# x1 transposed by VectorE in 32x32 blocks and sixteen SBUF transfers instead of by TensorE

## The reference

```python
x = L0_attn_x                                    # (16, 512, 256)
qkv = relu(x @ qkv_weight.T)                     # q, k, v: 32 heads of 8
vk = einsum('bnhe,bnhd->bhed', [v, 1], k)        # linear attention, per head
vk_q = einsum('bhed,bnhd->bnhe', vk, q)
att = vk_q[..., :8] / (vk_q[..., 8:] + 1e-15)
x1 = layernorm(x + att @ proj_weight.T + proj_bias)
h = silu(x1 @ (w_gate/127).T) * (x1 @ (w_up/127).T)      # hidden 768
out = layernorm(x1 + h @ (w_down/127).T)
```

## Time and profile before

| | |
|---|---|
| median of 3 runs | 555.05 us (554.89 to 556.29) |
| the profiled execution, its own time | 556.24 us |
| its span, first to last instruction | 554.4 us |
| mean granted TensorE clock | 0.995 |
| TensorE busy | 542.7 us (98%) |
| VectorE busy | 387.2 us (70%) |
| ACT busy | 221.3 us (40%) |
| GpSimd busy | 80.2 us (14%) |

### The profile page before, as it was taken

One profiled execution on the slowest core, in us unless ns is written; L12 is line 12 of the kernel. 1 busy time (PEld: TensorE's weight loads), 2 busy tenths in 40 slices (PEclk: granted clock), 3 DMA queues, 4 the chain that ended last, 5 costly groups with the idle time before them and its releaser, 6 DMA issues.

```text
span 554.4 us, 8767 instructions
## 1 busy us (share of the span) xinstructions
PE 542.7 (98%) x3275; PEld 480.0 (87%) x3275; DVE 387.2 (70%) x867; ACT 221.3 (40%) x376; POOL 80.2 (14%) x94
## 2 busy tenths in 40 slices
PE   8889999999999999999999999999999999999995
PEld 5778989898898988989898898988989898898975
DVE  5786758486684957758487684957858587684976
ACT  3356243543524445243542524445243442524431
POOL 1011110011110111110011110111110011100212
PEclk9999999999999999999999999999999999999999
DMA  8300121201111030121202112030121202102001
GB/s 302 154 0 2 39 77 40 76 0 76 38 38 76 0 113 0 38 76 38 76 0 76 38 38 76 0 113 1 38 76 38 76 0 76 38 0 77 2 39 38
DMA packets 8652, 29.02 MB, mean 52 GB/s; under 512 B 960, under 2 KB 1728, under 8 KB 8640
## 3 DMA queue, kind: packets, MB, share of 16 engines
q1 hardware_dynamic: 8640, 28.85, 14.4%
HBM read 20.46 MB, written 8.39 MB: 52 GB/s over the span
## 4 chain that ended last, share of the span: by engine, by line
PE 91%; DVE 4%; DMA 2%; ACT 1%; issue 1%; POOL 0%; SPq 0%; POOLq 0%
PE abcd_ps L580 48%; PE gate_ps L580 17%; PE up_ps L580 16%; PE abcd_ps L616 6%; PE abcd_ps L624 5%; DMA wg_raw<-w_gate 1%; DMA xT_raw<-x_chan 1%; DVE x1T_lo L336 0%; DVE h L343 0%; DVE xT_lo L336 0%; ACT silu L240 0%; DVE wg_lo L336 0%; DVE st L562 0%; DVE st L397 0%; DVE r L558 0%
## 5 line engine op out<-in xcount | busy, mean ns | idle before, releaser
L343 DVE SCALAR_TENSOR_TENSOR h<-up_ps,silu 128x512 f32<-128x512 f32 x96 | 66.0, 687 | 82.7 <-ACT silu L240 82.7
L240 ACT ACTIVATE silu<-gate_ps 128x512 f32<-128x512 f32 x96 | 57.4, 598 | 107.3 <-PE gate_ps L580 107.3
L580 PE MATMUL abcd_ps<-wd_hi,h_hi 128*128 128x256 f32 x384 | 93.1, 283 | 0.8 <-DVE h_lo L336 0.8
L580 PE MATMUL abcd_ps<-wd_hi,h_lo 128*128 128x256 f32 x384 | 92.9, 283 | 0.0
L580 PE MATMUL gate_ps<-x1T_hi,wg_hi 128*128 128x512 f32 x192 | 79.6, 415 | 2.0 <-DVE x1T_lo L336 1.9
L336 DVE TENSOR_TENSOR h_lo<-h,h_hi 128x512 fp32r<-128x512 f32 x96 | 65.9, 686 | 14.3 <-ACT h_hi L235 11.2
L580 PE MATMUL up_ps<-x1T_hi,wu_hi 128*128 128x512 f32 x192 | 75.7, 394 | 0.0
L580 PE MATMUL up_ps<-x1T_lo,wu_hi 128*128 128x512 f32 x192 | 75.6, 394 | 0.0
L580 PE MATMUL gate_ps<-x1T_lo,wg_hi 128*128 128x512 f32 x192 | 75.3, 392 | 0.0
L580 PEld LDWEIGHTS abcd_ps<-wd_hi,h_hi 128*128 128x128 f32 x384 | 73.7, 192 | 1.1 <-DVE h_lo L336 1.0
L580 PEld LDWEIGHTS abcd_ps<-wd_hi,h_lo 128*128 128x128 f32 x384 | 73.7, 192 | 0.0
(11 more groups left out here) (118 smaller groups left out, 968.9 us busy)
## 6 DMA issues: line engine op xcount, KB each, us to landing
x_raw<-x_tok SPq DMA_DIRECT2D x16, 512.0 KB, 3.3
xT_raw<-x_chan SPq DMA_DIRECT2D x15, 512.0 KB, 3.2
out<-out_sb SPq DMA_DIRECT2D x15, 512.0 KB, 2.6
wg_raw<-w_gate SPq DMA_DIRECT2D x1, 768.0 KB, 6.8
wu_raw<-w_up SPq DMA_DIRECT2D x1, 768.0 KB, 8.2
wd_raw<-w_down SPq DMA_DIRECT2D x1, 768.0 KB, 9.6
xT_raw<-x_chan SPq DMA_DIRECT2D x2, 256.0 KB, 3.4
wkv_raw<-w_kv SPq DMA_DIRECT2D x1, 512.0 KB, 5.1
```

Of the source, the lines that this page charges most:

```text
L240: nc.scalar.activation(silu[:, j % 2, :], gate_ps[j % 2][:], ACT.Silu, scale=WSCALE).then_inc(silu_ok[j], 1)
L343: nc.vector.scalar_tensor_tensor(out=h[:, j, :], in0=up_ps[j % 2][:], scalar=WSCALE, in1=silu[:, j % 2, :], op0=ALU.mult, op1=ALU.mult).th ...
L580: last = mm(dst, lhsT, rhs, start=start and n == 0, stop=stop and n == len(pairs) - 1)
```

## The change

For batches 1 to 14, x1 is no longer transposed by TensorE. VectorE writes x1 into a new buffer `x1n` (in the place of the raw gate weights, which are no longer needed), then transposes all of it in blocks of 32x32 in one instruction (`x1_squares`). Such a block stays in its 32 partitions, so 16 transfers, issued by SP in `spread_x1`, take the blocks from each of the four groups of 32 partitions to each of the four groups in `x1T_raw`: each has 32 partitions with two runs of 512 bytes, 32 KB. ACT and VectorE make `x1T_hi` and `x1T_lo` from there. A further transfer (`keep_x1`) copies x1n to x1 for the residual sum of the next pass, once r2 has been formed with the old one; r2's sum waits for it. On VectorE x1 and the block transpose come ahead of r2, `xT_lo` is cut in two with the aggregation between, and x1T_lo comes ahead of out_sb. On ACT x1T_hi stands behind the ReLU of tile 2. The tail's semaphores are merged into counting ones, to make room for the new ones. Batch 0 and batch 15 stay as they were.

```diff
+        def in_place_of(raw):
+            return raw[:].rearrange("p a b -> p (a b)")[:, 0:NT * C].bitcast(FP32)
+        x1n = in_place_of(wg_raw).rearrange("p (t c) -> p t c", t=NT)
+        x1_sq = in_place_of(wu_raw).rearrange("p (c t s) -> p c t s", c=NCB, t=NT)
+        x1T_raw = in_place_of(wd_raw).rearrange("p (k n) -> p k n", k=KC)
...
+        def x1T_spread(k):
+            return x1T_raw[:, k, :].rearrange("p (g t s) -> p t g s", g=NG, t=NT)
+        def by_token(T, k):
+            return T[:, k, :].rearrange("p (t g s) -> p t g s", g=NG, t=NT)
...
@@ SP
+            def spread_x1(b):
+                sp.wait_ge(x1_sq_ok, b)
+                for g in range(NG):
+                    for j in range(NG):
+                        sp.dma_start(x1T_raw[j * SQ:(j + 1) * SQ, :, g * P:(g + 1) * P],
+                                     x1_sq[g * SQ:(g + 1) * SQ, j::NG].rearrange("p k t s -> p k (t s)")).then_inc(x1T_in, 16)
+            def keep_x1(b):
+                sp.wait_ge(r2_ok[1], b)
+                sp.dma_start(x1[:], x1n[:]).then_inc(x1_copied, 16)
             def step(n):
...
                     load_xT(n + 1)
+                if any_n or 2 <= n < NB:
+                    spread_x1(n - 1)
+                    keep_x1(n - 1)
                 if any_n or n >= 2:
                     sp.wait_ge(out_ok, n - 1)
...
@@ ACT
+            def x1T_hi_spread(b):
+                act.wait_ge(up_mm[NH - 1], b)
+                act.wait_ge(x1T_in, 16 * NG * NG * b)
+                for k in range(KC):
+                    rounded(by_token(x1T_hi, k), x1T_spread(k), x1T_hi_ok[k])
...
-                x1T_hi_of(i)
                 if qkv:
                     kv_relu(2, i + 1, A)
+                    x1T_hi_spread(i)
                     kv_relu(3, i + 1, B)
...
@@ VectorE
+            def x1_new(b):
+                dve.wait_ge(rstd1_ok, b + 1)
+                if not isinstance(b, int) or b > 1:
+                    dve.wait_ge(x1_copied, 16 * (b - 1))
+                normed(x1n, r1, mv1, rstd1, x1_ok)
+            def x1_squares(b):
+                dve.wait_ge(x1_ok, b + 1)
+                nc.vector.transpose(x1_sq[:].rearrange("p c t s -> p t c s"),
+                                    x1n[:].rearrange("p t (c s) -> p t c s", s=SQ)).then_inc(x1_sq_ok, 1)
...
                 r1_of(i)
-                xT_lo_of(i + 1)
+                dve.wait_ge(xT_hi_ok, i + 2)
                 dve.wait_ge(st1_ok, i + 1)
+                minus_hi(xT_lo[:, 0, :], xT_raw[:, 0, :], xT_hi[:, 0, :])
+                aggregated(st1, mv1, mv1_ok)
+                minus_hi(xT_lo[:, 1, :], xT_raw[:, 1, :], xT_hi[:, 1, :]).then_inc(xT_lo_ok, 1)
+                x1_new(i)
+                x1_squares(i)
+                if not isinstance(i, int) or i > 1:
+                    dve.wait_ge(x1_copied, 16 * (i - 1))
                 r2_add(i - 1, 0, x1)
-                aggregated(st1, mv1, mv1_ok)
                 dve.wait_ge(r2_ok[0], i)
                 stats(st2, r2, 0)
                 r2_add(i - 1, 1, x1)
                 dve.wait_ge(r2_ok[1], i)
                 stats(st2, r2, 1, st2_ok)
                 dve.wait_ge(st2_ok, i)
-                x1_of(i, x1)
+                nc.vector.tensor_copy(st2_seen[:], st2[:, NT - 1, 0:1])
                 aggregated(st2, mv2, mv2_ok)
+                for k in range(KC):
+                    dve.wait_ge(x1T_hi_ok[k], i + 1)
+                    minus_hi(by_token(x1T_lo, k), x1T_spread(k), by_token(x1T_hi, k)).then_inc(x1T_lo_ok[k], 1)
                 out_of(i - 1)
-                x1T_lo_of(i)
...
@@ TensorE, last_part
-                pe.wait_ge(q_ok[KC - 1], i + 2)
-                x1T_of(i, x1)
                 for t in range(2, NT):
```

More of the change, by code:

```diff
@@ L23 @@
 NH = HID // P
+SQ = 32
+NG, NCB = P // SQ, C // SQ
 BANK = 512
@@ L92, in build @@
         ve2, rstd2 = sb("ve2", [P, NT]), sb("rstd2", [P, NT])
+        st2_seen = sb("st2_seen", [P, 1])
         out_sb, out_last = sb("out_sb", [P, NT, C]), sb("out_last", [P, NT, C])
@@ L119, in build @@
         x1T_mm, x1T_hi_ok, x1T_lo_ok = signals("x1T_mm", KC), signals("x1T_hi_ok", KC), signals("x1T_lo_ok", KC)
+        x1_sq_ok, x1T_in, x1_copied = signal("x1_sq_ok"), signal("x1T_in"), signal("x1_copied")
         gate_mm, up_mm = signals("gate_mm", NH), signals("up_mm", NH)
@@ L129, in build @@
         rstd1_pair, x1_pair = signals("rstd1_pair", 2), signals("x1_pair", 2)
-        down_tile, r2_tile, st2_tile = signals("down_tile", NT), signals("r2_tile", NT), signals("st2_tile", NT)
-        mv2_tile, ve2_tile = signals("mv2_tile", NT), signals("ve2_tile", NT)
-        rstd2_tile, out_tile = signals("rstd2_tile", NT), signals("out_tile", NT)
+        down_tile, r2_tile, st2_tile, mv2_tile, ve2_tile, rstd2_tile, out_tile = (
+            signal(f"{n}_tile") for n in ("down", "r2", "st2", "mv2", "ve2", "rstd2", "out"))
         last_down = [bank[:, :C] for bank in (A, B, CC, D)]
+        def x1T_spread(k):
+            return x1T_raw[:, k, :].rearrange("p (g t s) -> p t g s", g=NG, t=NT)
+        def by_token(T, k):
+            return T[:, k, :].rearrange("p (t g s) -> p t g s", g=NG, t=NT)
         def f32(tile):
@@ L178, in _ @@
             for t in range(NT):
-                sp.wait_ge(out_tile[t], 1)
+                sp.wait_ge(out_tile, t + 1)
                 sp.dma_start(out[NB - 1][:, t * C:(t + 1) * C], out_last[:, t, :]).then_inc(stored, 16)
@@ L225, in _ @@
             for t in range(NT):
-                rstd(0, mv2, mv2_tile[t], ve2, ve2_tile[t], rstd2, rstd2_tile[t], slice(t, t + 1))
+                rstd(t, mv2, mv2_tile, ve2, ve2_tile, rstd2, rstd2_tile, slice(t, t + 1))
         @block.scalar
@@ L313, in step @@
                     kv_relu(1, i + 1, B)
-                x1T_hi_of(i)
                 if qkv:
                     kv_relu(2, i + 1, A)
+                    x1T_hi_spread(i)
                     kv_relu(3, i + 1, B)
+                else:
+                    for k in range(KC):
+                        act.wait_ge(x1T_mm[k], 2)
+                        rounded(x1T_hi[:, k, :], (CC, D)[k], x1T_hi_ok[k])
             with act.Fori(1, NB - 1) as i:
@@ L556, in _ @@
             for t in range(NT):
-                dve.wait_ge(down_tile[t], 1)
+                dve.wait_ge(down_tile, t + 1)
                 nc.vector.scalar_tensor_tensor(
                     out=r2[:, t, :], in0=last_down[t], scalar=WSCALE,
[L560 to L564, removed]
+                    in1=x1_last[:, t, :], op0=ALU.mult, op1=ALU.add).then_inc(r2_tile, 1)
+                dve.wait_ge(r2_tile, t + 1)
+                nc.vector.bn_stats(st2[:, t, :], r2[:, t, :]).then_inc(st2_tile, 1)
+                dve.wait_ge(st2_tile, t + 1)
+                aggregated(st2, mv2, mv2_tile, (t,))
                 if t:
[L566 to L569, removed]
+                    dve.wait_ge(rstd2_tile, t)
+                    normed(out_last, r2, mv2, rstd2, out_tile, (t - 1,))
+            dve.wait_ge(rstd2_tile, t + 1)
+            normed(out_last, r2, mv2, rstd2, out_tile, (t,))
         @block.tensor
@@ L796, in _ @@
             for t in range(2):
-                down_part(i, t, range(NH - 1, NH), last_down[t]).then_inc(down_tile[t], 1)
+                down_part(i, t, range(NH - 1, NH), last_down[t]).then_inc(down_tile, 1)
             for t in range(2, NT):
-                down_part(i, t, range(NH), last_down[t]).then_inc(down_tile[t], 1)
+                down_part(i, t, range(NH), last_down[t]).then_inc(down_tile, 1)
 def kernel(L0_attn_x, L0_attn_qkv_weight, L0_attn_proj_weight, L0_attn_proj_bias,
```

## The result

The changed kernel takes 684.65 us, median of four runs (684.34 to 685.95), against 554.97 (554.56 to 556.29) for the kernel before on the same chip: 1.2336 times as long, 95% interval 1.231 to 1.2362. The forecast was 628 us with a range to 680. The direction held, the size did not: 130 us more in place of 73.

The account below looks back on a forecast made before the run. TensorE, busy 98% of the span, was taken as the bound. Each of 14 passes would be 3.6 us longer by waiting plus 1.6 for the clock: 73 us on the 555.05 median, 628 us; range 592 to 680.

Parts of the forecast that it names:

- What bounds the kernel, and where it would break: TensorE, busy 98%, bounds the kernel; it would wait about 4.5 us a pass for x1T_lo at the first gate matmul.
- What is taken away: TensorE's eight transposes of x1 in each loop pass: 14 x 0.87 us = 12.2 us saved.
- It just fits: r2's sum, behind the block transpose on VectorE, ends at 231.5, before TensorE's first kv matmul, due at 231.78.
- VectorE's part: On VectorE, x1 starts at 228.2 and ends at 229.6; block transpose takes 1.21 us, blocks ready at 230.8.
- the pitch of the issues: SP issues sixteen transfers 0.47 us apart (bounds 0.37 to 0.75), the first at 231.0, the sixteenth at 238.05.
- rival 2: Transfers on SP dearer than rows of long runs say, 0.71 us apart: 123 us more, 678 us; chance 0.24.
- Landing and the two rounding steps: Last transfer lands 1.7 us after issue (upper end 3.3); ACT's rounding and VectorE's subtraction take 1.97 us until the gate matmul.
- The clock: Behind TensorE's gate wait the granted clock falls to 0.50 in each pass, adding 1.6 us; lower end 0.
- The clock's upper end: 6.2 us of half speed, read from warm-up matmuls and one at 7.35 us taking 0.62 us, lose 2.9 us a pass.
- Rival 1: The wait at the gate comes but the clock holds: 14 x 3.6 us more, 605 us; chance 0.13.
- The covers: Copy of x1, ACT's fourth kv ReLU and the later load of x (covered by 2.5 us) cost nothing.
- Rival 3: Faster: SP issues at most 0.17 us apart, so no gate wait and the full 12.2 us gained, 543 us; chance 0.04.

Follow-up runs that it names:

- section 6: Versions of the changed kernel with five transfers through HBM (one store, four loads) instead of sixteen, first alone (615.15 us), then with successive reorderings (563.79, 564.58, 552.25, 556.6 us).
- the fourth section: Changed kernel, with TensorE running 30 matmuls of zeros into a free bank in the time it waits for x1T_lo: 653.88 us.
- four transfers: Changed kernel with four transfers of all 128 partitions instead of sixteen of 32, same bytes, blocks staying in their group of partitions: 569.31 us.
- the version with two queues: Reordered kernel with five transfers through HBM (563.79 us), fourth load issued by ScalarE instead of SP, att divided before the second h_lo is rounded: 564.58 us.
- the hop: Changed kernel with five transfers instead of sixteen: one stores the block-transposed tile to HBM, four load it back: 615.15 us.

## Why the prediction was right or wrong

- **What bounds the kernel, and where it would break**: right. TensorE was the bound, the wait came at the gate matmul, the last issue and not the last landing was what was late, and the clock fell behind it.
- **What is taken away**, 0.87 us a pass: wrong in what it is worth. With no transfers at all (and x1T_hi one ReLU earlier) 0.3 of it remains. "It just fits" was said of the kv matmul; it does not fit by 0.3 us.
- **VectorE's part**: x1 started at 228.80 on the old clock, not 228.2. Of the 0.6 us, 0.35 is GpSimd's small ve, which took 0.55 us beside VectorE's second half of xT_lo where it takes 0.20 alone; the prediction counted that half as free. The rest is gaps between instructions. The block transpose was 1.25 us against 1.21 assumed. First issue 0.49 us later than worked out.
- **The step that failed: the pitch of the issues**, "I take 0.47, the price in an unbroken row". The row was right about rows and wrong about kinds: its six issues all came from HBM, ours go from SBUF to SBUF with a split source, 0.64 us apart. 15 x 0.17 = 2.6 us a pass. The text had 0.71 as its upper bound, and rival 2 ("dearer transfers", 678 us, 0.24) is the case that came true. Its reason, two runs a partition, is half of it: two runs at the source do make an issue dear, two at the destination do not, and SBUF on both sides is enough without either.
- **Landing and the two rounding steps**: 1.86 against 1.7, 2.02 against 1.97.
- Together 0.49 + 2.57 + 0.16 + 0.05 = 3.3 us a pass, 46 of the 57 us that were missing.
- **The clock**, 1.6 us a pass: it fell in each pass as said, where the waits were 7.1 us, and cost 2.2 to 2.3. The forecast rested on a fall that was no rule: the wait of 1.57 us in batch 0 is in all fourteen kernels, and behind it the clock went to 0.50 in three (the kernel before and two of section 6) and stayed at 1.00 in eleven. The kernel after is one of these, at the place of the first row:

```profile
41.00:41.50 0.50, 0.50 (x4) 1.00 0.00 0
```

- **The clock's upper end**, 2.9 us, was misread: the 0.62 us at 7.35 in the earlier trace rows are two matmuls, which began 0.46 us after the two before them, so 0.23 us apart: full speed.
- **How long the clock stayed down**: it came back by about 251 in one pass and only near 210 in the pass before, whose wait ended at 203.41: passes alternate between 43.2 and 42.1 us. 0.7 x 14 = 10 us more than forecast, the rest. Rival 1 (the clock holds) fell with the rows of the clock and the fourth section.
- **The covers** of ACT's fourth ReLU, of the copy of x1 and of the load of x: held, the last because the pass grew.
- **Rival 3** needed issues 0.17 us apart; no issue in any run took less than 0.31. By the Trainium skill ("DMA: Bandwidth & Descriptors", Issuing engines are not separate DMA queues) the time to start a DMA is usually small beside the DMA itself. The trace differs: an issue holds the queue for 0.60 us and its transfer lands 1.86 us after the issue began, and the fifteen issues ahead of the last stand on the path in full.
- **The range** ended at 680 because its upper case held the pitch of 0.71 with the clock at 1.6. The measured 0.64 with 0.5 us of VectorE's and 0.7 of the clock's lateness comes out beyond it: three moderate misses of one sign, which the text called a rare coincidence.

## What to carry to other kernels

Count DMA issues on one queue as work of an engine: number times pitch, and take the pitch from a row with the same two memories and the same split of the source, or keep the dearest one as the forecast. Where a relay through transfers stands on the critical path, fewer and larger ones win even with a second landing (615 us against 685 here); and everything that stands behind them on the queue (a store, the next load) is late too, and may show only once the first wait is gone. An engine waiting for a transfer should do its other work ahead of that wait: moving out_sb there was worth some 12 us (564.58 to 552.25, ratios to the kernel before of 1.0175 and 0.9953), more than the idea itself. Part of the 2.4 us won in the end may come from the reordering rather than from the transposes; the reordering alone on the kernel before was not run.

## What was not expected of the hardware

- An issue on SP in a row takes 0.43 to 0.50 us for HBM to SBUF or back with a contiguous source, 0.60 to 0.65 us for SBUF to SBUF or a source in pieces of 512 bytes; 32 or 128 partitions make no difference (0.64 and 0.65). A lone load or store of 512 KB takes 0.33 to 0.36, a lone copy from SBUF to SBUF in one run 0.48.
- When GpSimd's 1024-wide addition (2.4 us) and a subtraction of two SBUF tiles on VectorE (0.69) overlap, the one that began later is stretched. In the pass shown the addition ran from 248.42 to 250.80; the subtraction began at 248.74 and ended at 251.35, 0.55 us after it, as in 67 of 69 such pairs in the traces. In eight passes of that run the subtraction began first, or 0.01 us after the addition; it kept its 0.68 and the addition took 2.8 to 2.9. A 4-wide addition on GpSimd that began behind a subtraction went from 0.20 to 0.55.
- Waits of TensorE of 1.18 us a pass (four transfers) left the clock at 0.998, and five of 1.4 to 1.7 us in the version with two queues left it at 0.999. Waits of 2.7 us a pass (the hop) lowered it in each pass. The wait of 1.57 us in batch 0 lowered it in three kernels of fourteen. Matmuls of zeros kept it up.
